# The last layer's four projection groups in a row on TensorE, ahead of the weighting of the values, in a three-layer attention kernel

## The chip, the cores and the metric

The kernel runs on one NeuronCore of a Trainium2 chip. The metric is the device time of one execution in microseconds. TensorE (PE in the profile) does the matrix products and can write only to PSUM; VectorE (DVE), ScalarE (ACT) and GpSimd (POOL) do the rest, SyncE (SP) issues the DMAs. Each engine works through its own queue in order and waits on semaphores for the others.

## The reference

Two layers of a decoder block (self-attention with a causal mask, cross-attention, a feed-forward part) and then one more cross-attention with rotary embedding. Everything is float32, with 32 sequences of 64 tokens, 128 features and 16 heads of 64. The last layer is the one that the change touches:

```python
q = (decoder_query @ Wq).reshape(B, Sq, H, Dh)
k = (encoder_key_value @ Wk).reshape(B, Skv, H, Dh)
v = (encoder_key_value @ Wv).reshape(B, Skv, H, Dh)
q = rope(q); k = rope(k)
scores = jnp.einsum('bhqd,bhkd->bhqk', q, k)        # q scaled by 1/sqrt(Dh)
attn = jax.nn.softmax(where(mask, scores, -1e9), axis=-1)
out = jnp.einsum('bhqk,bhkd->bqhd', attn, v).reshape(B, Sq, H * Dh) @ Wo
x = decoder_query + out
y = (x - mu) * rsqrt(var + 0.001) * ln_gamma + ln_beta
```

## The kernel before

**Units and steps.** Two sequences make a unit of 128 tokens. There are 16 units and 3 attention layers, so 48 units of work, and the program runs through steps u = -2 to 49. A step has several units in flight: the scores and the softmax of unit u, the transposed probabilities of an earlier unit, the weighting and the output product of unit u - 2, and the projection of Q (even u) or K (odd u) for a pair of units that comes later (`projected(u)`). The steps of the last layer's projections are u = 30 to 45 (`rotary`); in the same steps `by_head(u)` is true and the exponentials run head by head.

**The ring of banks.** PE's results other than the scores go through a ring of four PSUM banks, `ps_p`. The list `fills(u)` (L89) gives a step's fills in order; each names who empties it, "A" for ACT, "D" for DVE. Fill n goes into bank n mod 4, and `bank_free` (L523) makes PE wait until fill n - 4 has been emptied by those it names. PE, ACT and DVE all take their order from this list: PE walks through it, ACT walks through the entries with "A" (from L763, with the exponentials and `normalise_rest` put in between), and DVE has its own order (`vector_order`, L182), made from the entries with "D".

**One step of the last layer.** The fills are:
- PP0, PP1: the probabilities of unit u - 2 transposed by PE (L570), emptied by ACT into `probsT` (L680). From u = 33 on.
- FT, F1, F1, F2: the feed-forward part of the layer before, in odd steps up to 35 (so u = 31, 33, 35). F2 (L623) reads `hT`, which ACT writes (L691).
- Four projections "Qr" or "Kr": each is two heads-pairs' product, six matmuls of 256 columns (`split_product`, L439 to L441). DVE empties each by multiplying it with the rotary table into `turn` (L825), which has two buffers, and POOL adds the halves into `qT` or `kT` (L1046). DVE's third waits for POOL's first, its fourth for POOL's second (L800).
- O0, O1: the weighting of the values with the probabilities, `weight_values` (L498), 64 matmuls on L514 into two banks; it waits for `probsT` and for both banks. ACT empties them into `headsT` (L670). From u = 32 on they lie in the ring; before that in `ps_a`, and `heads` is empty in `fills`.
- V0, V1: the values of unit u, three matmuls of 512 columns each (L559 to L561), emptied by ACT (L678).
- Y: the output product (L598), which waits for `headsT`. DVE adds the residual into `z` (L847) and goes on to the statistics.
- T: the transposed input of the next pair (L547), in odd steps.

Ahead of the fills PE makes the scores of unit u (L467, L475), which wait for the exponentials of unit u - 1, and in even steps for POOL's rotary additions. In DVE's order a step is: maximum (L893), rotations one to four, first half of the normalisation (L938), `z` and statistics, sum (L921), reciprocal (L925), and the low half of T (L812). In ACT's order it is: PP0, PP1, first eight exponentials (L714), O0, O1, the other eight, V0, V1, the second half of the normalisation of unit u - 1 (L730), F1 or T.

Of the kernel before, what the change touches and what calls it, by code (L numbers as in the profile page):

```python
# [32 lines left out]
def projected(u):  # L33
    g = u // 2 + 1
    return g if g < N // 2 else None


def ffn_chunk(u):
    g = (u - 5) // 2
    return g if u % 2 and UNITS // 2 <= g < UNITS else None  # L40


def attends(u):
    return 0 <= u < N


def turns(u):
    return 0 <= u - 1 < N


def finishes(u):
    return 0 <= u - 2 < N


def rotary(u):
    return projected(u) is not None and projected(u) * 2 // UNITS == 2
# [7 lines left out]
def heads_in_ring(u):  # L64

    return finishes(u) and u >= 2 * UNITS
# [12 lines left out]
def by_head(u):  # L79

    return attends(u) and rotary(u)


def defers(u):

    return by_head(u) and u > 2 * UNITS - 1


def fills(u):  # L89

    heads = [("O", b, "A") for b in range(2)] if heads_in_ring(u) else []
    turn_in = [("T", 0, "AD")] if u % 2 == 0 and projected(u) is not None and not by_head(u) else []
    values = [("V", j, "A") for j in range(2)] if attends(u) else []
    probabilities = [("P", j, "A") for j in range(2)] if turns(u) and not defers(u) else []
    deferred = [("PP", j, "A") for j in range(2)] if defers(u - 1) else []
    result = [("Y", 0, "D")] if finishes(u) else []
    project = []
    if projected(u) is not None:
        name = "K" if u % 2 else "Q"
        for j in range(4):  # L100
            project.append((name + "r", j, "D") if rotary(u) else (name, j, "ADAA"[j]))
    late = u > 0 and u % UNITS == 0
    early, late = ([], values) if late else (values, [])
    next_in = [("T", 0, "AD")] if u % 2 and by_head(u + 1) else []
    if by_head(u):

        ffn = [("FT", 0, "AD")], [("F1", 0, "A"), ("F1", 1, "A")], [("F2", 0, "D")]
        into, inside, outof = ffn if ffn_chunk(u) is not None else ([], [], [])
        return deferred + into + project[:2] + heads + project[2:] + values + inside + result + probabilities + outof + next_in
    if ffn_chunk(u) is not None:  # L110
        k = len(project) // 2
        return heads + early[:1] + [("FT", 0, "AD")] + early[1:] + probabilities + project[:2] + [("F1", 0, "A")] \
            + project[2:k] + [("F1", 1, "D")] + project[k:] + [("F2", 0, "D")] + result + late + next_in
    if u % 2:
        return heads + early + probabilities + project + result
    k = len(project) // 2
    return deferred + heads + turn_in + early + probabilities + project[:k] + result + project[k:] + late
# [13 lines left out]


FILL = Tally(lambda u: [(n, j) for n, j, _ in fills(u)])
EMPTY_A = Tally(lambda u: [(n, j) for n, j, who in fills(u) if "A" in who])
EMPTY_D = Tally(lambda u: [(n, j) for n, j, who in fills(u) if "D" in who])
ALL_FILLS = [(u, n, j, who) for u in range(FIRST, END) for n, j, who in fills(u)]

# [1049 lines left out]
```

How the kernel before makes its waits and increments, by code:

```python
        @block.sync  # L386
# [20 lines left out]
            sp.dma_start(w1_raw, a["L0_xattn_ffn_w1"]).then_inc(w1_loaded, 16)  # L407
            sp.dma_start(w2[:, :, :], a["L0_xattn_ffn_w2"].rearrange("(c r) e -> r c e", r=128)).then_inc(late_loaded, 16)
            sp.dma_start(C[:, :, :], context).then_inc(late_loaded, 16)
            result = out.rearrange("(u b) s e -> (b s) u e", b=2)
            for u in range(1, END + 1):
                if u in (1, UNITS + 1):
                    layer = u // UNITS
                    for n in range(3):
                        sp.wait_ge(w_ready[n], parts_ready(layer, n))
                        sp.dma_start(w_raw[n][:, :], weight(layer + 1, "qkv"[n])).then_inc(w_loaded[n], 16)
                if u == UNITS + 3:
                    sp.wait_ge(filled, FILL.at(UNITS + 1, "Y", 0))
                    sp.dma_start(wo[:, 0, :, :], weight(2, "o").rearrange("(p r) e -> r p e", r=128)).then_inc(wo_loaded, 16)
                done = u - 3
                if 2 * UNITS <= done < N:
                    if by_vector(u - 1):
                        sp.wait_ge(dve_step, VSTEP.at(u - 1, "out"))
                    else:
                        sp.wait_ge(pool_step, PSTEP.at(u - 1, "out", 0))
                    v = done % 2
                    sp.dma_start(result[:, done % UNITS:done % UNITS + 1, :], y_out[:, v:v + 1, :]).then_inc(stored[v], 16)
            for v in range(2):
                sp.wait_ge(stored[v], 16 * UNITS // 2)
```

## Time and profile before

| | |
|---|---|
| Median of three runs | 554.58 us (554.28 to 556.31) |
| The profiled execution, time | 554.87 us |
| its span (first to last instruction) | 553.0 us |
| PE busy | 516.1 us, 93% |
| PE weight loads | 473.4 us, 86% |
| DVE busy | 419.6 us, 76% |
| ACT busy | 370.4 us, 67% |
| POOL busy | 290.5 us, 53% |
| Granted PE clock, mean | 0.996 |

The profile is a record of one execution. Times are microseconds from the start of the span; a row of the timeline is one instruction or several of one line merged (xN), with its start, how long it took, the engine, the line of the kernel, what it writes and reads, and in brackets how long the engine was idle before it and what ended that. A busy PE is not PE at its peak, since matmuls overlap and their ends are modelled: the distance from one start to the next tells what they cost.

The starts of PE's scores mark the steps: u = 32 begins at 361.47, u = 40 at 458.48, u = 41 at 468.50, u = 42 at 479.18.

### The profile page before, as it was taken

The page shows a single profiled execution, that of the slowest core. Times are in us where ns is not written, and L with a number is a line of the kernel's source. Part 1 is how long each engine was busy: PE and PEld are TensorE (multiplying, and loading weights), DVE is VectorE, ACT ScalarE, POOL GpSimd, SP SyncE. Part 2 cuts the span into 40 slices and gives each one's busy share as a digit, 9 for nine tenths or more (in the row PEclk, how much of TensorE's full clock was granted, in tenths as well). Part 3 has the DMA queues.
Part 4 walks back from the last instruction along what each step waited for, and adds up shares of the span by engine and source line. Part 5 has one row for each costly group of instructions (what it writes and reads, how often), then busy time and mean ns, then how long its engine had stood idle before and what let it go on. Part 6 is the DMA issues. An engine that isn't in the chain of part 4 may idle for free.

```text
span 553.0 us, 23802 instructions
## 1 busy us (share of the span) xinstructions
PE 516.1 (93%) x10364; PEld 473.4 (86%) x10364; DVE 419.6 (76%) x784; ACT 370.4 (67%) x1003; POOL 290.5 (53%) x563
## 2 busy tenths in 40 slices
PE   7899999999999899999999999888999999999885
PEld 6789898998988789898888988878888899999775
DVE  4777888767787577777777777887778888888843
ACT  6565766757767657645657575667676787887852
POOL 2214535454354354342624336868676787787724
PEclk9999999999999999999999999899999999999999
DMA  8900000000010110000000000000000000000000
GB/s 243 316 31 3 3 2 2 2 4 2 9 73 1 41 42 1 2 2 4 2 2 3 2 1 3 2 4 1 4 8 9 12 9 9 12 8 9 8 12 15
DMA packets 10838, 12.74 MB, mean 23 GB/s; under 512 B 752, under 2 KB 8432, under 8 KB 10736
## 3 DMA queue, kind: packets, MB, share of 16 engines
q1 hardware_dynamic: 10736, 11.24, 6.7%
q8 instruction: 82, 1.34, 1.1%
q14 instruction: 20, 0.16, 0.1%
HBM read 10.18 MB, written 1.05 MB: 20 GB/s over the span
## 4 chain that ended last, share of the span: by engine, by line
PE 77%; DVE 9%; ACT 6%; POOL 3%; issue 3%; DMA 1%; SPq 0%; POOLq 0%; ACTq 0%; DVEq 0%
PE ps_p L598 14%; PE ps_p L439 10%; PE ps_p L440 8%; PE ps_p L441 8%; PE ps_p L570 6%; PE ps_a L493 5%; PE ps_a L514 5%; PE ps_p L559 4%; PE ps_p L561 3%; PE ps_p L560 3%; PE ps_a L475 3%; PE ps_p L623 3%; PE ps_p L514 3%; DVE turn L825 2%; POOL kT L1046 2%
## 5 line engine op out<-in xcount | busy, mean ns | idle before, releaser
L1064 POOL TENSOR_TENSOR small<-mv,epsilon 128x1 f32<-128x1 f32 x48 | 18.1, 377 | 172.2 <-DVE mv L864 172.2
L598 PE MATMUL ps_p<-wo,headsT 128*128 128x128 f32 x768 | 93.6, 275 | 1.9 <-ACT headsT L670 1.3
L598 PEld LDWEIGHTS ps_p<-wo,headsT 128*128 128x128 f32 x768 | 90.5, 192 | 3.4 <-ACT headsT L670 1.4
L825 DVE TENSOR_TENSOR turn<-ps_p,rope 128x1024 f32<-128x1024 f32 x64 | 76.1, 1221 | 8.1 <-PE ps_p L441 5.6
L698 ACT ACTIVATE headsT<-ps_a 128x512 f32<-128x512 f32 x60 | 32.6, 596 | 69.0 <-PE ps_a L514 69.0
L921 DVE TENSOR_REDUCE total<-probs 128x16 f32<-128x1024 f32 x48 | 58.1, 1211 | 26.5 <-ACT probs L724 19.6
L680 ACT ACTIVATE probsT<-ps_p 128x512 f32<-128x512 f32 x96 | 52.9, 611 | 25.4 <-PE ps_p L570 25.3
L439 PE MATMUL ps_p<-xT_hi,wq_hi 128*128 128x256 f32 x192 | 60.0, 313 | 5.6 <-DVE xT_lo L812 2.9
L714 ACT ACTIVATE probs<-ps_a,top 128x64 f32<-128x64 f32 x256 | 55.9, 350 | 9.7 <-DVE top L893 7.3
L678 ACT ACTIVATE vv<-ps_p 128x512 f32<-128x512 f32 x96 | 57.2, 614 | 1.4 <-PE ps_p L561 1.0
L686 ACT ACTIVATE qT<-ps_p,columns 128x256 f32<-128x256 f32 x96 | 39.0, 489 | 27.3 <-PE ps_p L441 27.3
L897 DVE TENSOR_REDUCE top<-ps_a 128x8 f32<-128x512 f32 x64 | 41.2, 685 | 20.0 <-PE ps_a L493 19.9
L570 PE MATMUL ps_p<-eye,probs 128*128 128x128 f32 x384 | 53.5, 276 | 2.7 <-issue 2.2
L440 PE MATMUL ps_p<-xT_lo,wq_hi 128*128 128x256 f32 x192 | 54.2, 282 | 0.0
L441 PE MATMUL ps_p<-xT_hi,wq_lo 128*128 128x256 f32 x192 | 54.1, 282 | 0.0
L1046 POOL TENSOR_TENSOR qT<-turn 128x512 f32<-128x512 f32 x32 | 44.6, 1415 | 18.0 <-DVE turn L825 18.0
L570 PEld LDWEIGHTS ps_p<-eye,probs 128*128 128x128 f32 x384 | 43.2, 141 | 11.0 <-issue 4.7
L1046 POOL TENSOR_TENSOR kT<-turn 128x512 f32<-128x512 f32 x32 | 43.1, 1369 | 10.2 <-DVE turn L825 10.2
L439 PE MATMUL ps_p<-cT_hi,wk_hi 128*128 128x256 f32 x128 | 39.8, 311 | 5.2 <-ACT vv L678 3.2
L439 PEld LDWEIGHTS ps_p<-xT_hi,wq_hi 128*128 128x128 f32 x192 | 36.7, 191 | 9.3 <-issue 4.1
L938 DVE TENSOR_TENSOR probs<-probs,rinv 128x512 f32<-128x512 f32 x62 | 42.1, 682 | 0.0
L686 ACT ACTIVATE kT<-ps_p,columns 128x256 f32<-128x256 f32 x96 | 38.6, 479 | 4.6 <-PE ps_p L441 3.4
(138 smaller groups left out, 1392.8 us busy)
## 6 DMA issues: line engine op xcount, KB each, us to landing
out<-y_out SPq DMA_DIRECT2D x16, 64.0 KB, 1.6
X<-in_x SPq DMA_DIRECT2D x1, 768.0 KB, 8.3
across<-in_across SPq DMA_DIRECT2D x1, 704.0 KB, 10.0
wq_raw<-in_L_xattn_sa_wq SPq DMA_DIRECT2D x2, 256.0 KB, 3.7
wk_raw<-in_L_xattn_sa_wk SPq DMA_DIRECT2D x1, 512.0 KB, 5.6
wv_raw<-in_L_xattn_sa_wv SPq DMA_DIRECT2D x1, 512.0 KB, 7.6
wo<-in_L_xattn_sa_wo SPq DMA_DIRECT2D x1, 512.0 KB, 8.7
wo<-in_L_xattn_ca_wo SPq DMA_DIRECT2D x1, 512.0 KB, 9.6
```

Of the source, the lines that this page charges most:

```text
L439: mm(dst, w[0], x[0], start=True, stop=False)
L440: mm(dst, w[0], x[1], start=False, stop=False)
L441: return mm(dst, w[1], x[0], start=False, stop=True)
L570: last = nc.tensor.transpose(bank[:, 128 * pp:128 * pp + 128], probs[:, unit % 2, at_head:at_head + 2, :].rearrange("q h k -> q (h k)"), e ...
L598: last = mm(bank[:, 0:E], headsT[:, p, :, :].rearrange("r b q -> r (b q)"), wo[:, layer % 2, p, :], start=(p == 0), stop=(p == PAIRS - 1))
L678: ins = nc.scalar.activation(vv[:, u % 2, j, :, :].rearrange("k p d -> k (p d)"), bank[:, :], ACT.Copy)
L680: ins = nc.scalar.activation(probsT[:, j, :], bank[:, :], ACT.Copy)
L686: ins = nc.scalar.activation(to[:, g % 2, p, :], bank[:, CT * k:CT * k + CT], ACT.Identity, bias=bias[:, g * CU // UNITS, p:p + 1])
L714: ins = nc.scalar.activation(probs[:, u % 2, n, :], ps_a[:, bank, 64 * k:64 * k + 64], ACT.Exp, bias=top[:, at:at + 1], scale=scale)
L825: ins = V.tensor_tensor(turn[:, j % 2, :, :].rearrange("d a (h b t) -> d a h b t", h=2, t=S), bank[:, None, :].broadcast_to([128, 2, 512]) ...
L921: V.tensor_reduce(total[:, :], probs[:, u % 2, :, :], AX_X, ALU.add).then_inc(dve_step, 1)
L1046: G.tensor_tensor(to[:, projected(u) % 2, 2 * j:2 * j + 2, :], *turned(j), ALU.add).then_inc(rotated, 1)
```

## The change

One line of `fills`, for steps with `by_head(u)`: the four entries of `project` come in a row, and the two of `heads` behind them, in place of two, `heads`, two. Everything else, the orders of ACT and DVE included, is worked out from this list, and since neither swaps two entries that one engine empties, ACT's and DVE's own orders come out as before.

```diff
@@ -106,7 +106,7 @@
         ffn = [("FT", 0, "AD")], [("F1", 0, "A"), ("F1", 1, "A")], [("F2", 0, "D")]
         into, inside, outof = ffn if ffn_chunk(u) is not None else ([], [], [])
-        return deferred + into + project[:2] + heads + project[2:] + values + inside + result + probabilities + outof + next_in
+        return deferred + into + project + heads + values + inside + result + probabilities + outof + next_in
```

## Rows read from the trace of the kernel before

**Rows 1.** Busy time per stretch: stretch, its length, engines busy (instructions), PEclk, DMA

```profile
345.00:350.00 5.00, 3.31 (x141) 2.97 (x137) 4.93 (x8) 1.96 (x5) 4.48 (x8) 1.00 0.01 3
350.00:355.00 5.00, 5.00 (x26) 4.75 (x25) 4.67 (x7) 3.85 (x17) 2.95 (x4) 0.66 0.00 0
...
460.00:490.00 30.00, 29.65 (x715) 27.63 (x706) 25.41 (x34) 25.24 (x91) 23.33 (x30) 1.00 0.04 10
```

**Rows 2.** Waits from 437 to 520: who, for whom, total us, times, longest

```profile
DVE z L847 <- PE ps_p L598: 6.1, 8, 0.8
DVE turn L825 <- PE ps_p L441: 4.6, 12, 0.4
...
ACT probsT L680 <- PE ps_p L570: 13.0, 8, 1.8
```

**Rows 3.** Timeline, PE in step 41: start, us, engine, line, operation, [idle before]

```profile
468.50 0.32 PE L467 MATMUL ps_a<-mask,fold 32*64 32x256 bf16 x8
...
472.58 1.16 PE L514 MATMUL ps_p<-probsT,vv 64*64 64x64 f32 x64
...
473.67 0.39 PE L439 MATMUL ps_p<-cT_hi,wk_hi 128*128 128x256 f32 x1
...
475.27 0.39 PE L559 MATMUL ps_p<-wv_hi,cT_hi 128*128 128x512 f32 x1
...
476.67 1.95 PE L598 MATMUL ps_p<-wo,headsT 128*128 128x128 f32 x16
...
479.18 0.32 PE L467 MATMUL ps_a<-mask,fold 32*64 32x256 bf16 x8 [0.35 <-POOL kT L1046]
```

**Rows 4.** Timeline, DVE in step 41

```profile
468.61 0.29 DVE L847 TENSOR_TENSOR z<-ps_p,X 128x128 f32<-128x128 f32 x1 [0.74 <-PE ps_p L598]
...
472.04 2.36 DVE L825 TENSOR_TENSOR turn<-ps_p,rope 128x1024 f32<-128x1024 f32 x2
...
474.77 2.37 DVE L825 TENSOR_TENSOR turn<-ps_p,rope 128x1024 f32<-128x1024 f32 x2 [0.38 <-PE ps_p L441]
...
478.65 0.29 DVE L847 TENSOR_TENSOR z<-ps_p,X 128x128 f32<-128x128 f32 x1 [0.74 <-PE ps_p L598]
```

**Rows 5.** Timeline, POOL's first two rotary additions in step 41

```profile
473.35 2.54 POOL L1046 TENSOR_TENSOR kT<-turn 128x512 f32<-128x512 f32 x2 [0.83 <-DVE turn L825]
```

**Rows 6.** Timeline, step 35: first rotations, and PE (weight load, PEld) waiting

```profile
404.82 2.35 DVE L825 TENSOR_TENSOR turn<-ps_p,rope 128x1024 f32<-128x1024 f32 x2
...
407.22 0.19 PEld L439 LDWEIGHTS ps_p<-cT_hi,wk_hi 128*128 128x128 f32 x1 [0.29 <-DVE turn L825]
```

**Rows 7.** Timeline, DVE from step 39's residual into step 40

```profile
457.95 0.29 DVE L847 TENSOR_TENSOR z<-ps_p,X 128x128 f32<-128x128 f32 x1 [0.74 <-PE ps_p L598]
...
460.37 1.21 DVE L893 TENSOR_REDUCE top<-ps_a 128x16 f32<-128x1024 f32 x1
...
462.00 2.36 DVE L825 TENSOR_TENSOR turn<-ps_p,rope 128x1024 f32<-128x1024 f32 x2 [0.42 <-PE ps_p L441]
```

**Rows 8.** Timeline, DVE and PE in steps 32 to 35

```profile
369.87 2.49 DVE L825 TENSOR_TENSOR turn<-ps_p,rope 128x1024 f32<-128x1024 f32 x2
...
373.53 0.29 DVE L847 TENSOR_TENSOR z<-ps_p,res 128x128 f32<-128x128 f32 x1 [0.45 <-PE ps_p L598]
...
374.28 1.57 DVE L881 SCALAR_TENSOR_TENSOR X<-fz,frstd,across 128x128 f32<-128x128 f32 x2
...
378.59 2.35 DVE L825 TENSOR_TENSOR turn<-ps_p,rope 128x1024 f32<-128x1024 f32 x2
...
378.81 1.16 PE L514 MATMUL ps_p<-probsT,vv 64*64 64x64 f32 x64 [1.04 <-DVE x2T_lo L815]
...
401.49 0.59 DVE L881 SCALAR_TENSOR_TENSOR X<-fz,frstd,across 128x128 f32<-128x128 f32 x2
...
405.05 1.16 PE L514 MATMUL ps_p<-probsT,vv 64*64 64x64 f32 x64
...
413.72 2.02 PE L623 MATMUL ps_p<-w,hT 128*128 128x128 f32 x16 [0.92 <-ACT hT L691]
```

## The prediction

> **What bounds the kernel now.** I read the busy windows first, to see which engine paces the last layer and at which clock. In 30 us of it (460 to 490) TensorE (PE) is busy 29.65 us at full granted clock, VectorE (DVE) 25.41, ScalarE (ACT) 25.24 and GpSimd (POOL) 23.33 [rows 1]. Then the waits of the last layer's undisturbed part: DVE idles 6.1 us ahead of eight `z` additions because PE has not finished Y, and 4.6 us ahead of the rotations because PE has not finished the group, and ACT idles 13.0 us for the transposed probabilities [rows 2]. So PE paces it and the others have a little slack. Third, the timeline of one step (u = 41, PE starts it at 468.50), engine by engine, because the change only permutes PE's queue: the question is whether PE, in the new order, meets a bank that DVE has not emptied yet.
>
> Where things stand in that step: the weighting (64 small matmuls, L514) starts at 472.58, the second pair of projections at 473.67, V at 475.27, Y at 476.67, and the next step at 479.18 [rows 3]. DVE rotates the four groups in two pairs, 472.04 to 474.40 and 474.77 to 477.14, so about 1.18 us each, and adds `z` at 478.65 [rows 4]. PE makes one group in (475.27 - 473.67) / 2 = 0.80 us [rows 3]. That is the heart of it: DVE needs 1.18 us for what PE makes in 0.80.
>
> **The change, part by part.** The diff permutes `fills(u)`. For u = 30 and 31 `heads` is empty, so nothing changes; for the 14 steps u = 32 to 45 the weighting (banks O0, O1) goes from between the second and third projection to behind the fourth. No instruction is added or removed and no DMA moves. The order on ACT stays (it empties no projection of this layer), that on DVE stays (it empties no O), POOL's stays. What moves is PE's order and, with it, which earlier fill each of the four ring banks must be rid of:
> - third and fourth projection: before, banks of the first and second (DVE); now banks of PP0 and PP1 (ACT), or in u = 33 and 35 of PP1 and FT.
> - O0 and O1: before, banks of PP0, PP1; now of the first and second projection (DVE).
> - V0 and V1: before, banks of O0, O1 (ACT); now of the third and fourth projection (DVE).
>
> Can DVE start its rotations earlier, since the groups come sooner? The first two groups come as before. The third rotation also waits for POOL's addition of the first, because `turn` has two buffers: that addition starts at 473.35 and takes 2.54 / 2 = 1.27, so it ends at 474.62; the rotation started at 474.77 [rows 4, 5]. The gain is at most 0.1 us and the fourth rotation, which waits for POOL's next addition, gets none. I take nothing for it.
>
> So in u = 41, with 0.05 us from DVE's end to PE's start (407.17 to 407.22 where PE did wait for such a bank [rows 6]): PE has four groups by 472.58 + 1.60 = 474.18. The weighting waits for rotation two, 474.40 + 0.05 = 474.45, a stall of 0.3; it takes 473.67 - 472.58 = 1.09, to 475.54. V0 waits for rotation three, 474.77 + 1.18 + 0.05 = 476.00, a stall of 0.46, and takes (476.67 - 475.27) / 2 = 0.70. V1 waits for rotation four, 477.14 + 0.05 = 477.19, a stall of 0.49. Y starts at 477.89 in place of 476.67, and `z`, 1.98 us behind Y's start as now, comes at 479.87 in place of 478.65: **+1.22 us** [rows 3, 4]. In general: `z` comes 0.05 + 0.70 + 1.98 = 2.73 us behind the last rotation, where it now comes 1.51 us behind it. DVE's queue has `z` ahead of the sum, the reciprocal, the next maximum and the next rotations, so this delay goes round: rotations, V1, Y, `z`, maximum, rotations. DVE with its four rotations joins PE in the loop that sets the step, and the step cannot make the delay good.
>
> The 14 steps:
> - Seven steps (34, 36, 37, 39, 41, 43, 45) have DVE busy from `z` to the first rotation: each +1.22, together 8.54. Step 45's delay passes on through DVE to the tail.
> - Steps 38, 40, 42, 44: today the first rotation waits for PE. In u = 40, `z` at 457.95, maximum from 460.37 for 1.21, to 461.58, rotation at 462.00 [rows 7]. The maximum follows `z`, so with PE not late this 0.42 shrinks to the usual 0.07, and 0.35 comes back: 0.87 each (0.97 in u = 38, which waits less), together 3.58. Check: 1.22 + 0.87 = 2.09 on a pair that takes 468.61 - 457.95 + 478.65 - 468.61 = 20.70 now.
> - u = 32: DVE has the low half of wv between rotations two and three. Rotation four ends at 369.87 + 2.49 = 372.36, `z` moves from 373.53 to 375.09: +1.56 [rows 8].
> - u = 35: has the feed-forward part, and its last product waits for ACT (`hT`) [rows 8], whose queue follows the weighting: second exponential, V, the rest of the normalisation, `hT`. The weighting moves from 405.05 to 407.22 [rows 6, 8]: +2.17, all of it reaching the next step.
> - u = 33: the same, rotation two ends at 378.59 + 2.35 = 380.94, weighting 378.81 to 380.99, +2.18. But two small DVE operations (L881) took 1.57 us here, 0.59 in u = 34 [rows 8]. Here POOL was still adding rotary halves; once `z` is 1.56 later that is over, so up to 0.98 comes back. Ends 1.2 and 2.2; I take 1.2, as the second row is the undisturbed one.
>
> Sum: 8.54 + 3.58 + 1.56 + 2.17 + 1.2 = 17.05, or **17.1 us**. What hides the rest: ACT's queue moves back by 474.45 - 472.58 = 1.87 in u = 41 while the step moves by 1.22; the 0.65 between comes out of the 13.0 / 8 = 1.6 us that ACT waits per step ahead of the probabilities [rows 2], so it stays hidden. If that cover were gone it would cost up to 0.65 a step, 9 us in all. The profiled execution took 554.87 us, 0.29 above the median of the three runs; I add to the median: 554.58 + 17.1 = **571.7**. It is 3.1%, against about 0.5% that a measurement of this kernel can tell from no change.
>
> The Trainium skill (Perfetto Trace Analysis, section Matmuls) advises to let independent matmul groups rotate through different banks, so that the evacuation of one lies beside the next group's matmuls. Both orders do rotate through four banks, and by that rule the sum would be near 0. The rows speak against it for this order: a rotation of four banks hides 1.18 us behind 0.80 only while other fills, emptied by ACT, stand between the groups.
>
> **The rivals.**
> - *The emptying stays hidden* (the other side, 554). It would be so if DVE had the second rotation done by the time PE has four groups (474.18) and the fourth when PE has V0 without a stall (474.18 + 1.09 + 0.70 = 475.97). The place is the three bank waits ahead of O, V0 and V1; the price of 17.1 us disappears if DVE runs 1.2 us earlier in the step. For it: DVE idles 0.74 ahead of `z`. Against it: that idle time ends with PE's Y, so an earlier start of DVE needs an earlier Y, and the rows put rotation four at 477.14. Were it so, the third rotation's 0.1 us would be the whole effect: 554 to 554.6. Chance 0.05.
> - *Less, because the steps take up part.* If the four groups in a row let DVE and POOL run the rotations at their own pace (4 x 1.18 without the 0.37 gap in the middle), each step pays 0.85 in place of 1.22: 14 x 0.37 = 5 less, 567. Against it: the gap ends with POOL as much as with PE. Chance 0.10.
> - *More, through ACT or PE's clock.* The granted clock was 0.66 in 350 to 355, behind a stretch in which PE was busy 3.31 of 5 us [rows 1]: 0.34 x 5 = 1.7 us a time. In the new plain steps PE is busy some 10 of 11.3 us, but the steps with feed-forward stall for 2 us twice; two to four falls, or ACT's cover gone in part, give 575 to 581. Chance 0.12.
> - Forecast, with errors of 0.1 to 0.2 us in the terms of 14 steps: 569 to 575. Chance 0.73.
>
> **How the numbers follow.** The likeliest case gives 571.7. With the ends for unknown costs (u = 33, ACT's cover, less gap) and the two neighbouring cases in part, 8 in 10 lies in 565 to 580. Slower by over 0.5%: 0.94; within 0.5%: 0.04; faster: 0.02, both from the first rival, since nothing in the order promises PE less work.
>
> **What would show it.** In the changed kernel's waits, PE should wait for DVE `turn` ahead of L514 (0.3 us a step) and twice ahead of L559 (0.5 each), some 17 us with the steps 33 and 35; the wait of DVE `turn` for PE L441 should vanish; a pair of steps should take 22.8 us; the distance from the last rotation's end to `z` should be 2.73 us. The steps up to 361 us should be the same. The prediction is wrong if PE shows no wait on `turn`, if the third rotation starts clearly earlier behind the second, or if the granted clock drops in the last third.

## The result, and the profile after

| | before | changed |
|---|---|---|
| Median | 554.62 us (4 runs) | 575.17 us (4 runs, 572.71 to 577.72) |
| Ratio, 95% interval | | 1.0355 (1.0323 to 1.0386) |
| The same in a later job | 555.08 us (18 runs, 552.95 to 557.5) | 573.63 us (4 runs, 573.52 to 574.59) |
| Ratio, 95% interval | | 1.0338 (1.0310 to 1.0366) |
| Profiled executions, time | 554.87 | 577.72, and 573.68 in the later job |

The change costs 19 to 20 us by the ratios, 3.4 to 3.5%. First the head of the page of the changed kernel (the execution of 577.72 us): engine, busy time, share, instructions.

```profile
span 575.8 us, 23802 instructions
## 1 busy us (share of the span) xinstructions
PE 527.7 (92%) x10364; PEld 478.8 (83%) x10364; DVE 419.6 (73%) x784; ACT 372.2 (65%) x1003; POOL 289.4 (50%) x563
```

The instructions are the same in number and DVE's busy time is the same to 0.1 us. PE's busy time grew from 516.1 us to 527.7 here and to 521.9 in the later job's profile, which has fewer falls of the clock. The rest of what grew is waiting. The waits of the changed kernel from 361 to 545 us, its steps 32 to 45 (who, for whom, total, times, longest):

```profile
DVE z L847 <- PE ps_p L598: 32.4, 14, 3.5
ACT headsT L670 <- PE ps_p L514: 29.5, 14, 3.0
...
PEld ps_p L559 <- DVE turn L825: 13.7, 25, 0.7
...
PE ps_p L514 <- DVE turn L825: 7.4, 13, 0.9
...
PE ps_p L559 <- DVE turn L825: 6.1, 24, 0.3
...
DVE turn L825 <- POOL kT L1046: 1.8, 7, 0.3
DVE turn L825 <- POOL qT L1046: 1.6, 6, 0.3
```

PE now waits for DVE's rotations ahead of the weighting (L514) and ahead of V (L559), which it did not in the undisturbed steps before [rows 2]; DVE's wait for PE's projections [rows 2, 4] is gone. DVE waits for PE more than before (ahead of `z`), and PE for DVE: a loop of both. The step that answers to [rows 3, 4] is this one, u = 41 (timeline, DVE and PE; start, duration):

```profile
482.56 0.29 DVE L847 TENSOR_TENSOR z<-ps_p,X 128x128 f32<-128x128 f32 x1 [2.16 <-PE ps_p L598]
...
484.90 0.37 PE L439 MATMUL ps_p<-cT_hi,wk_hi 128*128 128x256 f32 x1
...
485.99 2.36 DVE L825 TENSOR_TENSOR turn<-ps_p,rope 128x1024 f32<-128x1024 f32 x2
...
487.75 0.28 PE L441 MATMUL ps_p<-cT_hi,wk_lo 128*128 128x256 f32 x1
488.49 1.16 PE L514 MATMUL ps_p<-probsT,vv 64*64 64x64 f32 x64 [0.45 <-DVE turn L825]
488.60 2.46 DVE L825 TENSOR_TENSOR turn<-ps_p,rope 128x1024 f32<-128x1024 f32 x2 [0.26 <-POOL kT L1046]
...
489.88 0.50 PE L559 MATMUL ps_p<-wv_hi,cT_hi 128*128 128x512 f32 x1 [0.23 <-DVE turn L825]
...
491.12 0.50 PE L559 MATMUL ps_p<-wv_hi,cT_hi 128*128 128x512 f32 x1 [0.28 <-DVE turn L825]
...
491.92 1.95 PE L598 MATMUL ps_p<-wo,headsT 128*128 128x128 f32 x16
...
493.90 0.29 DVE L847 TENSOR_TENSOR z<-ps_p,X 128x128 f32<-128x128 f32 x1 [2.17 <-PE ps_p L598]
```

Rotation two ends at 485.99 + 2.36 = 488.35, and the weighting starts 0.14 later; rotation four ends at 488.60 + 2.46 = 491.06 and V1 starts at 491.12. From one `z` to the next it is 11.34 us, where it was 478.65 - 468.61 = 10.04 [rows 4]. The loop can be added up: from `z` to the first rotation 485.99 - 482.56 = 3.43 us, as before; the four rotations 5.07, before 5.10; from the last rotation's end to the next `z` 2.84, before 1.51. The whole growth of the step lies in the last of the three.

Where the 22.8 us between the two profiled spans (552.98 and 575.84) lie: 2.0 ahead of step 32 (it starts at 363.49 in place of 361.47), 17.8 from there to the `z` of step 45, 3.0 behind it, all of it in steps 46 and 47. Most of the first and the last part goes with PE's clock: 1.6 of the 2.0 come in the step with a fall at 188 us (the other 0.4 are there before the first `z`), and there is a fall in step 46 and one in step 47. Busy time per stretch in the changed kernel (stretch, length, PE, PEld, DVE, ACT, POOL, granted clock, DMA):

```profile
187.00:192.00 5.00, 5.00 (x24) 4.41 (x24) 1.71 (x3) 4.42 (x9) 0.14 (x1) 0.66 0.01 3
...
365.00:370.00 5.00, 3.23 (x35) 3.04 (x29) 4.84 (x8) 1.75 (x8) 1.04 (x2) 0.86 0.00 0
370.00:375.00 5.00, 4.44 (x78) 3.51 (x78) 4.97 (x5) 2.06 (x8) 4.84 (x6) 0.80 0.02 5
...
545.00:550.00 5.00, 4.83 (x77) 4.03 (x78) 0.81 (x1) 3.48 (x8) 0.00 (x0) 0.66 0.06 15
555.00:560.00 5.00, 3.71 (x26) 2.91 (x27) 1.76 (x4) 2.78 (x6) 1.50 (x4) 0.66 0.06 16
```

In these stretches part of the time is granted at 1.2 in place of 2.4 GHz. The profile of before had one such place ahead of its end [rows 1]. The experiment `after_again` tells which of them come again.

### The profile page after: what moved, and what is told of

It is laid out like the page before. It is cut to its first block, busy times and chain, and to the rows that moved or that the text cites. A ratio compares the mean times of both kernels' runs of the same rounds, so it can differ in the third digit from the quotient of the medians.

```text
span 575.8 us, 23802 instructions
## 1 busy us (share of the span) xinstructions
PE 527.7 (92%) x10364; PEld 478.8 (83%) x10364; DVE 419.6 (73%) x784; ACT 372.2 (65%) x1003; POOL 289.4 (50%) x563
## 4 chain that ended last, share of the span: by engine, by line
PE 70%; DVE 13%; ACT 6%; POOL 6%; issue 3%; DMA 1%; POOLq 0%; ACTq 0%; SPq 0%; DVEq 0%
PE ps_p L598 14%; PE ps_p L439 8%; PE ps_p L440 6%; PE ps_p L441 6%; PE ps_p L570 6%; DVE turn L825 6%; PE ps_a L493 5%; PE ps_a L514 5%; PE ps_p L559 4%; POOL qT L1046 3%; PE ps_p L561 3%; PE ps_p L560 3%; PE ps_p L623 3%; PE ps_a L475 2%; PE ps_a L486 2%
## 5 line engine op out<-in xcount | busy, mean ns | idle before, releaser
L440 PE MATMUL ps_p<-xT_lo,wq_hi 128*128 128x256 f32 x192 | 55.6, 289 | 0.0
L441 PE MATMUL ps_p<-xT_hi,wq_lo 128*128 128x256 f32 x192 | 55.5, 289 | 0.0
L570 PEld LDWEIGHTS ps_p<-eye,probs 128*128 128x128 f32 x384 | 44.4, 143 | 11.5 <-issue 5.3
L670 ACT ACTIVATE headsT<-ps_p 128x512 f32<-128x512 f32 x36 | 19.6, 596 | 41.4 <-PE ps_p L514 41.4
L439 PEld LDWEIGHTS ps_p<-xT_hi,wq_hi 128*128 128x128 f32 x192 | 38.2, 199 | 9.6 <-issue 4.4
L938 DVE TENSOR_TENSOR probs<-probs,rinv 128x512 f32<-128x512 f32 x62 | 43.3, 701 | 0.0
L439 PE MATMUL ps_p<-cT_hi,wk_hi 128*128 128x256 f32 x128 | 38.6, 302 | 5.0 <-ACT vv L678 3.2
```

Source lines behind the costliest of these rows:

```text
L439: mm(dst, w[0], x[0], start=True, stop=False)
L440: mm(dst, w[0], x[1], start=False, stop=False)
L441: return mm(dst, w[1], x[0], start=False, stop=True)
L570: last = nc.tensor.transpose(bank[:, 128 * pp:128 * pp + 128], probs[:, unit % 2, at_head:at_head + 2, :].rearrange("q h k -> q (h k)"), e ...
L938: V.tensor_tensor(p, p, factor[:, 8 * j:8 * j + 8, None].broadcast_to([128, 8, S]), ALU.mult)\
```

## The experiments

My theory: the new order makes PE wait for DVE's rotations, because O0, O1, V0 and V1 now take the banks of the four projections. Rivals: the weighting's lateness delays ACT's queue; POOL and the two buffers of `turn` set the pace; PE's clock. Ratios are to the kernel before, run on the same chip in the same job. "Plain steps" are 38 to 45, and their times are from one `z` to the next, for odd and for even u; before they took 10.04 and 10.66 us (10.55 in u = 38), in the changed kernel 11.35 and 11.64.

**The changed kernel once more** (`after_again`, no edit).

> The changed kernel once more, for the falls of the granted clock. Its first profile took 577.72 us with five falls of 3.4 us at half clock (at 188, 352, 369, 546 and 556 us), one of them 175 us ahead of the first changed step; before had two (350 and the end). If the falls are chance beside the change, this profile has other places and another number of them, the time of a profile goes with their number (1.5 to 2 us each), and with only one ahead of the end it takes about 573. If the changed steps cause them, they lie at 369, 546 and 556 again.

Measured: 573.63 us, ratio 1.0338 (1.0310 to 1.0366), and the profiled execution took 573.68. Ahead of the end its clock fell at 350 us and 544 us only; the falls at 188, 369 and 556 were not there. Its steps 32 to 45 cost 17.8 us over before, as in the first profile, and 1.1 us more come behind step 45, and its plain steps took 11.34 and 11.64. The stretches:

```profile
350.00:355.00 5.00, 5.00 (x26) 4.73 (x26) 4.67 (x7) 3.93 (x17) 3.03 (x4) 0.68 0.00 0
535.00:540.00 5.00, 5.00 (x162) 4.68 (x163) 2.73 (x7) 4.11 (x17) 2.90 (x6) 1.00 0.02 3
540.00:545.00 5.00, 2.30 (x70) 1.81 (x69) 2.87 (x4) 3.71 (x12) 1.74 (x4) 0.94 0.06 16
545.00:550.00 5.00, 5.00 (x34) 4.40 (x33) 1.47 (x2) 3.56 (x7) 0.00 (x0) 0.72 0.00 0
```

A fall in step 46 makes that step some 12.3 us from `z` to `z` in place of 10.7 (13.6 in one profile in which it lasted twice as long). It was there in ten of the fourteen profiles of this study, `quads` with the old order among them; four had none, before, `turn4_two_two`, `half_four` and `four_exp`, two of them with the new order. So the falls do not need the change, and those at 188, 369 and 556 us come and go between two profiles of one program. For step 46 it is less clear. Ahead of its weighting PE waits 2.7 us for `probsT` in both profiles of the changed kernel, and 2.1 us before. Of the eleven profiles with a wait of 2.5 to 2.7 us nine have the fall, of the three with 2.1 us one has it. The change may thus make that fall likelier, by way of the wait; no run here shows it.

**Three groups ahead, one behind** (`three_one`).

```diff
-        return deferred + into + project[:2] + heads + project[2:] + values + ...
+        return deferred + into + project[:3] + heads + project[3:] + values + ...
```

> Three groups ahead of the weighting, one behind it. Bank-wait theory: in a plain step the weighting needs only the first rotation (done at 4.70 us of the step, before PE has its three groups at 4.86), the fourth group waits for the second rotation (5.95), V0 for the third (about 7.45, no longer for ACT), V1 for ACT's O0. V0 and V1 run 7.5 to 8.9, Y starts at 8.9 in place of 8.15: +0.75 a step, in all 14 steps some 9 to 12 us: 564 to 567. If the delay came from the weighting's own lateness (ACT's chain behind it, which is late by 0.8 of the 1.9 us), it would be about 0.8/1.9 of the whole, 8 to 9 us. If PE's clock or the order as such were the cause, no such split follows and it may lie anywhere from 555 to 575.

Measured: 564.40 us, ratio 1.0170 (1.0140 to 1.0199), about half of the whole. Plain steps 10.80 and 11.11. Timeline, PE in step 40:

```profile
469.10 1.16 PE L514 MATMUL ps_p<-probsT,vv 64*64 64x64 f32 x64
470.19 0.39 PE L439 MATMUL ps_p<-xT_hi,wq_hi 128*128 128x256 f32 x1
...
471.62 0.50 PE L559 MATMUL ps_p<-wv_hi,cT_hi 128*128 128x512 f32 x1 [0.44 <-DVE turn L825]
...
473.13 1.95 PE L598 MATMUL ps_p<-wo,headsT 128*128 128x128 f32 x16
```

The weighting has no wait, V0 waits for the third rotation, and Y starts at 473.13 - 464.11 (the step's start) = 9.02 us, where I had put 8.9. The size could have come from ACT's lateness as well (8 to 9 us was the rival's), but the place of the wait could not.

**Only the steps with the feed-forward part** (`ffn_only`).

```diff
+        k = 4 if u in (33, 35) else 2
-        return deferred + into + project[:2] + heads + project[2:] + values + ...
+        return deferred + into + project[:k] + heads + project[k:] + values + ...
```

> The new order in steps 33 and 35 alone (those with the feed-forward part). Bank-wait theory with ACT's chain behind the weighting: 1.2 to 2.2 us and 2.2 us, so 558.0 to 559.0. If all steps paid alike (the whole over 14), 2.9 us: 557.5. If only V1's wait counted (1.2 each), 557.0.

Measured: 559.18 us, ratio 1.0075 (1.0048 to 1.0101), so 4.2 us with an interval of 2.7 to 5.6. The times don't tell 2.9 from 4.4. The trace says more: the intervals that end with the `z` of steps 33, 34, 35 and 36 are longer by 0.92, 0.69, 1.29 and 0.67 us, 3.6 together, and those of 37 to 45 are as before. That lies in the 3.4 to 4.4 of the bank waits with ACT's chain behind them; the first of the four is the least sure, since steps 32 and 33 differ by some tenths between profiles of the old order.

**Half the rotation, in both orders** (`half_two_two`, `half_four`). DVE multiplies with the cosine half only, so these kernels leave out the sine part of the rotary embedding and serve to measure time alone. In the lines not shown the sine half of `turn` is set to zero once at the start.

```diff
-                    ins = V.tensor_tensor(turn[:, j % 2, :, :].rearrange("d a (h b t) -> d a h b t", ...),
-                                          bank[:, None, :].broadcast_to([128, 2, 512]) ...,
-                                          rope[:, "QK".index(name[0]), :, None, :] ..., ALU.mult)
+                    ins = V.tensor_tensor(turn[:, j % 2, 0, :].rearrange("d (h b t) -> d h b t", h=2, t=S),
+                                          bank[:, :].rearrange("d (h b t) -> d h b t", h=2, t=S),
+                                          rope[:, "QK".index(name[0]), 0:2, None, :].broadcast_to([128, 2, 4, S]), ALU.mult)
```

> Order of before, but DVE multiplies each projection with the cosine half of the rotary table only (half the elements, some 0.6 us in place of 1.18; the sine half is left out and POOL adds zeros, so q and k of the last layer are wrong by that part). PE set the pace before, so little changes: POOL's last addition comes earlier, which frees 0.35 us in seven even steps: 551 to 554.6.

> The new order with the same halved rotation (sine half left out). Bank-wait theory: rotations two and four now end about when PE has four groups and V0, so the plain steps lose their delay; steps 33 and 35 keep 1 to 1.4 us each since the weighting still comes 1.4 us later there and ACT's chain follows it. ACT's queue, 1.5 us later in each step with no growth of the step to cover it, may add up to 0.3 a step. Difference to the two-two order with the same halving: 2 to 6 us, in place of 18 to 20. If the cause is the late weighting alone, or PE's order, or the clock, the difference stays at 15 us or more.

Measured: 552.51 us, ratio 0.9954 (0.9936 to 0.9973), and 561.36 us, ratio 1.0107 (1.0068 to 1.0146). The difference falls from 19 or 20 us to 8.9, so more than half of the cost is gone, but it misses my 2 to 6. Plain steps: 9.99 and 10.28 with two and two, 10.40 and 10.71 with four. The timeline of `half_four`, step 41, shows what came in its place:

```profile
477.19 0.69 DVE L825 TENSOR_TENSOR turn<-ps_p,rope 128x512 f32<-128x512 f32 x1 [0.69 <-POOL kT L1046]
...
478.43 0.69 DVE L825 TENSOR_TENSOR turn<-ps_p,rope 128x512 f32<-128x512 f32 x1 [0.55 <-POOL kT L1046]
...
479.17 0.51 PE L559 MATMUL ps_p<-wv_hi,cT_hi 128*128 128x512 f32 x1
```

The halved rotations wait for POOL's additions, since `turn` has two buffers, and V1 follows the last of them (478.43 + 0.69 = 479.12). So I made `turn` larger.

**Four buffers of turn** (`turn4_two_two`, `turn4_four`, `turn4_half_four`).

```diff
-        turn = sb("turn", [128, 2, 2, 512])
+        turn = sb("turn", [128, 4, 2, 512])
-                    if j >= 2:
-                        dve.wait_ge(rotated, ROTATED.at(u, name, j - 2))
-                    elif ROTATED.before(u):
+                    if ROTATED.before(u):
                         dve.wait_ge(rotated, ROTATED.before(u))
```

(`turn[:, j % 2, ...]` is `turn[:, j, ...]` in DVE's and POOL's instructions.)

> Order of before, but turn has four buffers in place of two, so no rotation waits for POOL. PE made the third group only as POOL finished its first addition, so nothing should move: 554 to 556, and the wait of DVE turn for POOL is gone.

> The new order with four buffers of turn. The four rotations should now run without the gap of 0.26 us in the middle, V1 and z come 0.25 to 0.35 us sooner in each step: 4 to 5 us less than the new order, so 568.5 to 570, and 13 to 15 us over the same buffers with the two-two order. If the delay were POOL's (the two buffers) and not DVE's 1.18 us per rotation, the new order would be as fast as the old one here, 555 to 557.

> The new order, the halved rotation (sine half left out) and four buffers of turn. The halved rotation alone left some 0.4 us in each plain step, where V1 waits for a rotation that waits for POOL's addition. Bank-wait theory: this is the rest, and the plain steps now take as long as with the two-two order and the halved rotation (10.0 and 10.3 us); only steps 33 and 35 with their successors keep theirs: 2 to 4 us over 552.5, 554 to 557. If the 0.4 is ACT's queue or the weighting's place, it stays: 559 to 562.

Measured:

| | order | rotation | us | ratio (95%) | plain steps |
|---|---|---|---|---|---|
| `turn4_two_two` | two, two | full | 554.68 | 0.9986 (0.9966 to 1.0006) | 10.04, 10.67 |
| `turn4_four` | four | full | 569.70 | 1.0260 (1.0221 to 1.0298) | 10.9 to 11.2, 11.2 to 11.5 |
| `turn4_half_four` | four | half | 561.96 | 1.0114 (1.0087 to 1.0141) | 10.35, 10.74 |

With full rotations it came as expected: the old order gains nothing, the new one 4 us, and it stays 15 us slower. POOL and the two buffers are a small part. The 15 us that stay are not DVE's alone, though: ACT's wait ahead of the transposed probabilities is down from 4.6 us in seven plain steps (changed kernel) to 1.7, and the steps grow from 10.9 to 11.2 us as they go on. With half rotations it did not come as expected: the steps did not fall. The timeline of `turn4_half_four` (a step's start is 473.17) shows a third engine:

```profile
475.58 0.25 DVE L921 RECIPROCAL inv<-total 128x16 f32<-128x16 f32 x1 [0.35 <-ACT probs L730]
475.62 0.63 PE L570 MATMUL ps_p<-eye,probs 128*128 128x128 f32 x4 [0.18 <-ACT probs L730]
...
480.27 1.09 ACT L670 ACTIVATE headsT<-ps_p 128x512 f32<-128x512 f32 x2 [1.52 <-PE ps_p L514]
```

No wait of PE for a rotation is left in the plain steps, nor one of DVE for POOL, but ACT sits 1.5 us ahead of O0, comes late to the second half of the normalisation (L730), and both the reciprocal and the next transposes wait for that. It is the cover that the prediction named (1.6 us of ACT's waits per step); with a step that grows by 0.4 us only it is used up: ACT's waits for the transposes come to 0.8 us in seven steps.

**ACT's exponentials ahead of O0** (`turn4_half_four_exp`, `four_exp`). `turn4_half_four` and the changed kernel, with this in ACT's loop:

```diff
-                        while waiting and ((name, j) == ("V", 0) or (name, j) == ("O", 0) and len(waiting) == 2):
+                        while waiting and (name, j) in (("V", 0), ("O", 0)):
                             exponentials(u, waiting.pop(0))
```

> The new order, halved rotation (sine half left out), four buffers of turn, and ACT makes all sixteen exponentials ahead of emptying O0 and O1, which it waits 1.5 us a step for. With the banks no longer the bound, the plain steps still took 10.36 and 10.74 us, and DVE's reciprocal and PE's transposes waited for ACT's normalisation. If ACT's queue behind the late weighting is the second cost, the normalisation now comes about 1.5 us sooner, the plain steps fall to 10.0 and 10.3 as in the two-two order, the first product F2 comes sooner too: 553 to 556. If it is something else (PE's order, a matmul's cost), the steps stay at 10.4 to 10.7: 560 to 562.

> The new order with full rotations and two buffers, and the same change of ACT's order. In the plain steps the banks are the bound and ACT is not, so they stay at 11.35 and 11.64 us; steps 33 and 35 lose part of their wait ahead of F2, 0.7 to 1.5 us each: 571 to 572.5 beside 573.6 for the new order. If ACT's late queue were the main cost of the new order, it would fall to below 565.

Measured: `turn4_half_four_exp` 553.42 us, ratio 0.9977 (0.9957 to 0.9998), plain steps 9.99 and 10.31, against 9.99 and 10.28 in the two-two order with half rotations. `four_exp` 571.65 us, ratio 1.0331 (1.0259 to 1.0402), plain steps 11.36 and 11.64, as in the changed kernel. Timeline, step 41 of the first and step 35 of the second:

```profile
471.24 1.16 PE L514 MATMUL ps_p<-probsT,vv 64*64 64x64 f32 x64
472.33 0.50 PE L559 MATMUL ps_p<-wv_hi,cT_hi 128*128 128x512 f32 x1
473.14 0.40 PE L559 MATMUL ps_p<-wv_hi,cT_hi 128*128 128x512 f32 x1
473.83 1.95 PE L598 MATMUL ps_p<-wo,headsT 128*128 128x128 f32 x16
```

```profile
417.08 1.53 ACT L691 ACTIVATE hT<-ps_p,columns 128x256 f32<-128x256 f32 x4
418.76 2.02 PE L623 MATMUL ps_p<-w,hT 128*128 128x128 f32 x16 [0.93 <-ACT hT L691]
```

So four groups in a row cost nothing in the plain steps with all three edits: rotations of 0.7 us, a `turn` that never waits, and an ACT queue that makes its exponentials in place of waiting for the weighting. The two-two order with the same three edits was not run, but it could hardly be faster in these steps: PE is busy for 71.00 of 71.00 us both in `half_two_two` (446 to 517) and in `turn4_half_four_exp` (445 to 516). Over all of the intervals 32 to 45 the two profiles differ by 0.7 us, 158.9 and 159.6. The two stretches, in that order (stretch, length, PE, PEld, DVE, ACT, POOL, granted clock, DMA):

```profile
446.00:517.00 71.00, 71.00 (x1787) 66.08 (x1786) 51.22 (x80) 60.01 (x215) 56.99 (x78) 1.00 0.04 10
```

```profile
445.00:516.00 71.00, 71.00 (x1788) 65.50 (x1787) 49.79 (x80) 59.54 (x215) 56.60 (x78) 1.00 0.04 10
```

Whether the four buffers are needed beside ACT's order is open: alone they took nothing off `half_four`, and half rotations with ACT's order and two buffers were not run. With full rotations ACT's order alone does nothing in the plain steps; PE's wait ahead of F2 is 0.93 us, where the changed kernel has 1.62:

```profile
421.69 2.02 PE L623 MATMUL ps_p<-w,hT 128*128 128x128 f32 x16 [1.62 <-ACT hT L691]
```

**A finer wait in the old order** (`quads`, `rest_late_quads`). Both start from the kernel before; the second empties F1 on ACT ahead of the second half of the normalisation.

```diff
-                    pe.wait_ge(rotated, ROTATED.before(u))
+                    pe.wait_ge(rotated, ROTATED.before(u) - 3)
                     for quad in range(H // 4):
+                        if v == 0 and quad:
+                            pe.wait_ge(rotated, ROTATED.before(u) - 3 + quad)
```

```diff
-                        if by_head(u - 1) and (name, j) == ("V", 1):
+                        if by_head(u - 1) and (name, j) == (("F1", 1) if ffn_chunk(u) is not None else ("V", 1)):
```

> The kernel before, in which PE's scores of even steps (32 to 46) wait for POOL's rotary additions quad by quad instead of for all four at the start: the first quad waits for the first addition, the last for the last. Today PE waits 0.35 us for the last addition in each such step; with the wait behind three quarters of the scores it should vanish: 7 or 8 times 0.35 to 0.5 is 2.5 to 4 us less, 551 to 552. The rival: DVE, whose residual addition then comes sooner but whose maximum is followed by the same rotations, sets the pair of steps, and nothing is gained (554 to 555).

> The two-two order with scores waiting quad by quad, and in the steps with the feed-forward part ACT empties F1 ahead of the second half of the normalisation, not behind it. hT is then ready 2.0 us sooner and PE's wait of 0.9 to 1.1 us ahead of F2 should vanish in steps 33 and 35 (and 31, if it waits there): 2 to 3 us less, with 1.3 from the scores 551 to 552.5 beside 555 of before. The rival: the normalisation, now 1.5 us later, keeps the next step's transposes or reciprocal waiting and gives it back, 554 to 555.

Measured: `quads` 556.02 us, ratio 1.0007 (0.9986 to 1.0029); its even plain steps take 10.33 in place of 10.66, but only steps 38, 40, 42 and 44 gain, 1.2 us in all, and that is not seen in the times. I had counted seven or eight steps; 34 and 36 have another bound. `rest_late_quads`: 554.15 us, ratio 0.9977 (0.9957 to 0.9996): the intervals behind steps 33 and 35 are 0.95 us shorter each, and the kernel is 1.3 us faster than before by the times (0.2 to 2.4), less than I expected. It is the one version with the whole computation that beats both kernels beyond its interval, and only just.

## Why the prediction was right

I forecast 571.7 us (565 to 580), slower by 3.1%, and 575.2 and 573.6 were measured. By the steps of the prediction:

- **PE set the pace and DVE needs 1.18 us for what PE makes in 0.80.** Right, and the cause: with rotations of 0.7 us and ACT and `turn` freed the new order costs nothing in the plain steps. The full cost of the new order is 19 or 20 us, and half the rotation leaves 8.9. The four buffers alone take nothing off that; ACT's order on top of them takes off nearly all of it.
- **The waits in step 41** were put at 0.3, 0.46 and 0.49 us. The changed kernel shows 0.45, 0.23 and 0.28 of PE idle, each ended by a rotation as worked out. The first is longer than mine: four groups in a row take PE 3.0 us from the first start (484.90 to 487.75, and 0.12 for the last matmul by the spacing of its neighbours), where the rows of before, with the weighting in between, gave 3.2. The other two are shorter than mine; the profile lets a matmul's modelled end run into the gap. Taken together the forecast had 17 us of such waits in the 14 steps, and the profile shows 7.4 + 6.1. The starts agree: the weighting 5.93 us behind the last `z` (5.84 forecast: 474.45 - 468.61), Y 9.36 (9.28).
- **+1.22 in odd and +0.87 in even plain steps.** Measured 1.31 and 0.98. The term that was too small is V1: its first matmul takes 0.50 us behind the wait in place of 0.39, and V1 lasts 491.92 - 491.12 = 0.80 in place of 0.70. A pair of steps takes 22.98 us, 22.8 forecast. `z` comes 493.90 - 491.06 = 2.84 us behind the last rotation, where I had 2.73.
- **Third rotation at most 0.1 earlier.** It starts 488.60 - 485.99 = 2.61 behind the first, before 474.77 - 472.04 = 2.73, and the fourth waits for POOL, so nothing of it reaches `z` but 0.03.
- **Steps 32 to 36.** By PE's step starts 32 grew by 1.64 (1.56 forecast), 33 by 1.01 (1.2), 34 to 36 together by 4.59 (4.61). That last match is partly luck: one by one they grew by 1.31, 1.99 and 1.29, where I had 1.22, 2.17 and 1.22. The choice of the lower end for step 33 holds: L881 took 0.59 us there in the changed kernel, with POOL's rotary addition over before it began, and in the kernel before 1.57, beside one. Within the step the weighting moved by 6.69 - 5.40 = 1.29 us in step 33, and by 2.27 in step 35.
- **The sum**: 17.05 forecast for steps 32 to 45 and what they pass on, 17.8 in both profiles. The steps 37 to 45 make the difference, 10.6 for 9.7.
- **What hides ACT's delay.** Right for the changed kernel: `four_exp` frees ACT and the plain steps do not move. ACT's wait ahead of the transposed probabilities fell from 1.6 to 0.7 us a step. That the cover is thin is right as well: in `turn4_half_four` it was all but gone, and the step was 0.4 us longer.
- **The clock.** The sum had no term for it. The rest between 17.8 and the 19 to 20 us measured is not explained by the changed steps; 5.0 us in the first profile and 1.1 in the second lie outside them, most of it in steps with a fall. I had placed the danger in the feed-forward steps, and the ones that cost time came in steps 46 and 47 and once 175 us ahead of the change. The one at 369 us, in step 32, cost nothing that shows: the interval is 16.52 us with it and 16.55 in `after_again` without it. The prediction also named a drop of the clock in the last third as a sign that it is wrong. By its words that sign came, at 544 or 546 us in both profiles; it was badly chosen, since three kernels with the old order have the same fall, and it leaves the changed steps as they are.
- **The rule on banks.** The rule of the Trainium skill (Perfetto Trace Analysis, section Matmuls) on rotating through banks was not enough here: both orders rotate through four banks, and they differ by 17.8 us in the changed steps. What decided was which engine has to empty the bank that comes up again.
- **The rivals.** "The emptying stays hidden" fell. The runs show one way to make it come true in the plain steps: rotations of 0.7 us, four buffers of `turn` and ACT's changed order. "Less" had the right part (the gap between the rotations is worth 4 us when taken away with four buffers) but the changed kernel has the buffers it has. "More, through ACT or the clock" came in part, through the clock; whether by chance or by the longer wait in step 46 is open.

## What to carry to other kernels

In a ring of PSUM banks, write beside each fill who empties the fill that had its bank before, and how long that engine takes for one against PE's time for one. Here four groups of one slow engine in a row filled the whole ring of four and cost 19 to 20 us, three in a row cost 9, and with two and two PE has no such wait in the plain steps: fills of another engine between them are what hides the emptying. And when a queue is freed of its bound, look for the next in line before the gain is booked; here DVE's rotation was worth 0.9 us of the 1.3 in an odd plain step, and the last 0.4 went only when ACT's order was changed as well.

## What the runs showed of the hardware that was not expected

A matmul of 512 columns that follows a wait, or follows the 64 small matmuls of the weighting, takes 0.50 us in the record and pushes the next by 0.1 us; in an unbroken row it takes 0.39 or 0.40. A rotation of half the elements (128x512 out of PSUM) takes DVE 0.69 us in place of 1.18, so by my estimate (2 x 0.69 - 1.18) 0.2 us of each do not shrink with the size. Two small DVE operations (L881) took 1.57 us beside an addition on POOL and 0.59 without one. And a fall of the granted clock to 1.2 GHz in step 46 came in ten of fourteen profiles, with either order. It makes that interval 1.6 us longer, of which the next step gives some back, so that single profiles of this kernel can differ by 1 to 1.6 us for it.
